# A graph network layer on one core: first edge layer in fp32 on 64 array rows per edge half, and its activation moved two units ahead of the messages

## What is computed

```
h    = relu(layernorm(x))                                  # per node
e    = relu(raw @ W_e1.T + b_e1) @ W_e2.T + b_e2           # per edge, raw has 64 features
edge = (e * (clip(polarity, 0, 1) + 0.01)) @ W_le.T + b_le
msg  = relu(h[src] + edge)
aggr = segment_sum(msg, dst)
u    = (h + aggr) @ W_g1.T + b_g1 ; layernorm with gain and bias ; relu
out  = x + u @ W_g2.T + b_g2
```

## Time and profile before

| | |
|---|---|
| median of 3 runs | 2511.51 us (2511.22 to 2516.98) |
| the profiled execution, its own time | 2513.17 us |
| its span in the profile | 2511.5 us |
| mean granted TensorE clock | 0.991 of full |
| PE busy | 2341.1 us, 93% |
| DVE busy | 1904.1 us, 76% |
| ACT busy | 1586.8 us, 63% |
| POOL busy | 1644.0 us, 65% |
| moved by DMA | 349.07 MB, mean 139 GB/s |

### The profile page before, as it was taken

The page is one execution under the profiler, slowest core; times in us unless marked ns, Lnnn a source line. Parts: engine busy times, 40 slices in busy tenths (PEclk is TensorE's granted clock), DMA queues, the critical chain, the costliest instruction groups (busy, mean ns, idle before and its releaser), DMA issues.

```text
span 2511.5 us, 34919 instructions
## 1 busy us (share of the span) xinstructions
PE 2341.1 (93%) x10492; PEld 1946.3 (77%) x10492; DVE 1904.1 (76%) x3747; ACT 1586.8 (63%) x3112; POOL 1644.0 (65%) x1679
## 2 busy tenths in 40 slices
PE   5798999999999999999999999999999999999998
PEld 4677787877887787778877787877787787787876
DVE  7677777877787777777777777777787777777776
ACT  7566666666666666666666666666666666666664
POOL 6666666666666666666666666666666666666663
PEclk9899999999999999999999999999999999999999
DMA  9444444444444444444444444444444444444442
GB/s 311 131 132 129 132 146 131 139 130 134 145 140 136 131 145 139 135 133 141 139 136 133 133 135 143 134 137 132 137 143 137 134 134 143 137 137 134 141 140 60
DMA packets 136344, 349.07 MB, mean 139 GB/s; under 512 B 32019, under 2 KB 58325, under 8 KB 136149
## 3 DMA queue, kind: packets, MB, share of 16 engines
q0 software_dynamic: 77376, 211.39, 29.6%
q1 hardware_dynamic: 58772, 135.37, 15.8%
HBM read 333.82 MB, written 12.82 MB: 138 GB/s over the span
## 4 chain that ended last, share of the span: by engine, by line
PE 50%; DVE 27%; another core or an unknown queue 9%; issue 9%; ACT 4%; POOL 1%; DVEq 0%; DMA 0%; ACTq 0%; SPq 0%
PE bank L828 29%; DVE bank L676 11%; PE bank L844 9%; DVE mhl L686 7%; PE bank L806 5%; DVE oh L665 4%; PE bank L807 4%; DVE rlo L427 3%; ACT mhl L601 1%; PE bank L875 1%; PE bank L861 1%; ACT rhi L422 1%; POOL x_sba L371 1%; ACT hh L589 1%
## 5 line engine op out<-in xcount | busy, mean ns | idle before, releaser
L578 POOL DMA_INDIRECT hx<-gather_table,sidx x1612 | 1604.9, 996 | 823.7 <-issue 400.6
L828 PE MATMUL bank<-wc,hh 128*128 128x256 f32 x6448 | 1467.2, 380 | 2.7 <-issue 2.5
L828 PEld LDWEIGHTS bank<-wc,hh 128*128 128x128 f32 x6448 | 1218.9, 191 | 179.8 <-issue 9.2
L601 ACT ACTIVATE mhl<-bank 128x512 fp32r<-128x512 f32 x806 | 482.3, 599 | 842.1 <-DVE bank L676 671.7
L676 DVE SCALAR_TENSOR_TENSOR bank<-bank,gt,hx 128x256 f32<-128x256 f32 x1612 | 683.0, 484 | 380.1 <-remote 311.1
L686 DVE SCALAR_TENSOR_TENSOR mhl<-bank,mhl 128x512 fp32r<-128x512 f32 x806 | 549.7, 689 | 26.8 <-ACT mhl L601 1.8
L806 PE MATMUL bank<-rhi,w1r 128*128 128x512 f32 x806 | 379.8, 471 | 129.2 <-ACT hh L589 81.7
L589 ACT ACTIVATE hh<-bank 128x512 f32<-128x512 f32 x806 | 441.2, 601 | 28.2 <-remote 19.4
L594 ACT COPY bank<-c 128x512 f32<-128x512 f32 x802 | 450.5, 609 | 0.0
L844 PE MATMUL bank<-mhl,oh 128*128 128x512 f32 x1612 | 444.0, 397 | 0.5 <-DVE mhl L686 0.5
L665 DVE TENSOR_TENSOR oh<-iota,slot 128x512 fp32r<-128x512 f32 x403 | 279.2, 693 | 138.6 <-PE bank L844 80.7
(11 more groups left out here) (93 smaller groups left out, 479.7 us busy)
## 6 DMA issues: line engine op xcount, KB each, us to landing
raw<-in_attr_m SPq DMA_DIRECT2D x202, 512.0 KB
hx<-gather_table,sidx POOLq DMA_INDIRECT x1612
x_sba<-in_x SPq DMA_DIRECT2D x12, 512.0 KB, 8.9
gather_table<-x_sba SPq DMA_DIRECT2D x12, 512.0 KB, 7.7
xt<-in_x SPq DMA_DIRECT2D x48, 128.0 KB
out<-xt SPq DMA_DIRECT2D x48, 128.0 KB
dst_i<-in_dst_m SPq DMA_DIRECT2D x1, 805.5 KB
sidx<-in_src_m SPq DMA_DIRECT2D x1, 805.5 KB
```

The source lines that it names most:

```text
L578: eng.indirect_dma_start(out=hx[:, u % NX, j, :], out_offset=None, in_=tables, in_offset=bass.IndirectOffsetOnAxis(ap=sidx[:, t:t + 1], ax ...
L601: eng.activation(mh[:, u % 2, 2 * q:2 * q + 2, :], LB[(2 * u + q) % 4][:, :].rearrange("p (j n) -> p j n", j=2), ACT.Relu).then_inc(r_mh, 1)
L828: last = eng.matmul(o, hh[:, u % 2, k, e0:e0 + P], wc[:, k, :], start=False, stop=(j == 1 and k == 1), skip_group_check=seeded)
```

## The change

The first layer is done in fp32 from the raw values. A unit's 512 edges lie as two halves of 256: the features of half 0 on rows 0 to 63, those of half 1 on rows 64 to 127. Four matmuls of 256 columns with 64 rows each replace the four of 512 columns with 128 rows; the halves alternate, and each half has a bank of its own. The two roundings (lines 422 and 427) go, with their tiles. The bias enters in the activation, which becomes four instructions of 256 columns. One load of raw values is one unit, and eight are kept. On ACT `hidden_high(u+2)` stands at the head of iteration u, and the seed of unit u+2 behind the messages of unit u. Some preparation of weights is gone, and the constant of the place at which SP handles a node tile is new.

```diff
-NR = 3
+NR = 8
-NM = 4
...
-                eng.wait_ge(s_w, 16 * len(loads))
-                eng.wait_ge(s_m, 6)
-                eng.tensor_copy(w1r[0:F, 0, :], w1[0:F, :])
-                eng.tensor_copy(w1r[F:P, 1, :], w1[F:P, :])
...
-        raw = sb("raw", [P, NR, 1024], F32, early)
-        rhi = sb("rhi", [P, NM, 512], F32R, early)
-        rlo = sb("rlo", [P, NM, 512], F32R, early)
+        raw = sb("raw", [P, NR, 256], F32, early)
...
-        def load_raw(eng, n):
-            eng.dma_start(raw[:, n % NR, :], attr_m[n, :, :]).then_inc(r_load[n % NR], 16)
-
-        def raw_high(eng, u):
...
-            eng.copy(rhi[:, u % NM, :], part(u)).then_inc(r_rh, 1)
-
-        def raw_low(eng, u):
...
-            eng.tensor_tensor(rlo[F:P, u % NM, :], part(u)[F:P], rhi[F:P, u % NM, :].bitcast(F32),
-                              ALU.subtract).then_inc(r_rl, 1)
+        def load_raw(eng, u):
+            eng.dma_start(raw[:, u % NR, :], attr_m[u, :, :]).then_inc(r_load[u % NR], 16)
...
-                hh = sb("hh", [P, 2, 2, 512], F32, c)
+                hh = sb("hh", [P, 2, 2, 2, D], F32, c)
...
-                    place = {(GU * g + 23) // 2: t for g, t in TILE_AFTER.items()}
+                    place = {GU * g + 27: t for g, t in TILE_AFTER.items()}
...
-                    for n in range(NR, (UNITS + 1) // 2):
-                        eng.wait_ge(r_rl, 2 * (n - NR) + 2)
+                    for n in range(NR, UNITS):
+                        eng.wait_ge(r_l1, 2 * (n - NR) + 2)
...
-                        for k in range(2):
-                            eng.wait_ge(r_l1, 2 * u + k + 1)
-                            eng.activation(hh[:, u % 2, k, :], LA[k][:, :], ACT.Relu).then_inc(r_hh, 1)
+                        for q in range(2):
+                            eng.wait_ge(r_l1, 2 * u + q + 1)
+                            for k in range(2):
+                                last = eng.activation(hh[:, u % 2, q, k, :], LA[q][:, D * k:D * k + D], ACT.Relu,
+                                                      bias=b1[:, k:k + 1])
+                            last.then_inc(r_hh, 1)
...
                     for u in range(UNITS):
-                        if u + 3 < UNITS:
-                            raw_high(eng, u + 3)
-                        if u + 1 < UNITS:
-                            hidden_high(u + 1)
+                        if u + 2 < UNITS:
+                            hidden_high(u + 2)
...
-                        if 1 <= u < UNITS - 1:
-                            seed(u + 1)
                         message_high(u, 0)
                         message_high(u, 1)
+                        if u + 2 < UNITS:
+                            seed(u + 2)
...
                     def first_layer(u):
-                        eng.wait_ge(r_rl, u + 1)
...
+                        loaded(eng, u)
+                        if u >= 1:
+                            eng.wait_ge(r_hh, 2 * (u - 1) + 2)
                         for k in range(2):
-                            if u >= 1:
-                                eng.wait_ge(r_hh, 2 * (u - 1) + k + 1)
-                            eng.matmul(LA[k][:, :], w1r[:, 0, k * P:k * P + P], rhi[:, u % NM, :], start=True, stop=False)
-                            eng.matmul(LA[k][:, :], w1r[:, 1, k * P:k * P + P], rlo[:, u % NM, :],
-                                       start=False, stop=True).then_inc(r_l1, 1)
+                            for h in range(2):
+                                last = eng.matmul(LA[h][:, D * k:D * k + D], w1[F * h:F * h + F, k * P:k * P + P],
+                                                  raw[F * h:F * h + F, u % NR, :], start=True, stop=True)
+                                if k == 1:
+                                    last.then_inc(r_l1, 1)
```

More of the change, by code:

```diff
@@ L158, in gpsimd @@
                 eng.wait_ge(s_z, 3)
-                eng.wait_ge(s_m, 6)
+                eng.wait_ge(s_m, 5)
                 eng.wait_ge(s_io, 2)
@@ L404, in gnn @@
         early = ExitStack()
[L405 to L428 removed]
+        raw = sb("raw", [P, NR, 256], F32, early)
+        def loaded(eng, u):
+            eng.wait_ge(r_load[u % NR], 16 * (u // NR + 1))
+        def load_raw(eng, u):
+            eng.dma_start(raw[:, u % NR, :], attr_m[u, :, :]).then_inc(r_load[u % NR], 16)
         def nodes_again():
@@ L536, in _ @@
                     load_raw(eng, 0)
+                    load_raw(eng, 1)
                     for g in b["stores"](eng):
@@ L540, in _ @@
                         if g == LATE:
-                            load_raw(eng, 1)
-                    load_raw(eng, 2)
+                            load_raw(eng, 2)
+                            load_raw(eng, 3)
+                    for u in range(4, NR):
+                        load_raw(eng, u)
                     eng.dma_start(wg1[:, :, :], W_g1T.rearrange("(k p) n -> p k n", p=P)).then_inc(s_wg, 16)
@@ L628, in _ @@
                     for g in b["scalar"](eng):
-                        if g == SPLIT:
-                            for u in range(2):
-                                raw_high(eng, u)
+                        pass
+                    eng.wait_ge(a["s_w"], a["n_w"])
                     eng.wait_ge(s_o1, 16 * FIRST)
                     hidden_high(0)
-                    raw_high(eng, 2)
-                    eng.wait_ge(s_wt, 2)
+                    hidden_high(1)
+                    eng.wait_ge(s_wt, 1)
                     for u in range(UNITS):
-                        if u + 3 < UNITS:
-                            raw_high(eng, u + 3)
-                        if u + 1 < UNITS:
-                            hidden_high(u + 1)
+                        if u + 2 < UNITS:
+                            hidden_high(u + 2)
                         t = TILE_AFTER.get(u // GU - 1)
@@ L739, in _ @@
                         pass
-                    raw_low(eng, 0)
-                    raw_low(eng, 1)
                     own = a["edges"](eng)
@@ L747, in _ @@
                         pass
-                    raw_low(eng, 2)
                     eng.wait_ge(s_sl, 1)
+                    eng.wait_ge(s_o1, 16 * FIRST)
                     onehot(0)
@@ L825, in second_layer @@
                                 o = LB[(2 * u + q) % 4][:, D * j:D * j + D]
-                                e0 = (2 * q + j) * P
                                 for k in range(2):
-                                    last = eng.matmul(o, hh[:, u % 2, k, e0:e0 + P], wc[:, k, :],
+                                    last = eng.matmul(o, hh[:, u % 2, q, k, j * P:j * P + P], wc[:, k, :],
                                                       start=False, stop=(j == 1 and k == 1), skip_group_check=seeded)
@@ L1205 @@
     p = "L0_gnn_"
-    tiles = (E + 1023) // 1024
-    attr_m = _np.zeros((tiles, P, 1024), _np.float32)
-    wide = _np.zeros((F, tiles * 1024), _np.float32)
+    wide = _np.zeros((F, UNITS * 512), _np.float32)
     wide[:, :E] = w["edge_attr_65"][:, 1:].T
-    attr_m[:, 0:F, :] = wide.reshape(F, tiles, 1024).transpose(1, 0, 2)
-    attr_m[:, F:P, :] = attr_m[:, 0:F, :]
+    attr_m = wide.reshape(F, UNITS, 2, 256).transpose(1, 2, 0, 3).reshape(UNITS, P, 256)
     data = [
```

20 lines of the change are left out of this document (removed).

## The result

The changed kernel takes **2636.5 us** (2632.7 to 2640.2, 4 runs), the kernel before 2512.9 us (2511.2 to 2517.0, 4 runs): ratio 1.0489, 95% interval 1.0468 to 1.0511. It is slower by 124 us. 2480 us was forecast, with a range of 2395 to 2720.

What follows compares the result with a forecast made beforehand. PE was taken as the bound, 93% busy. Passes removed -371, new passes +435, shape changes +20, idle -115 sum to -31 us: from 2513.2 to 2482 profiled, 2480 us as median; range 2395 to 2720, its own 2400 to 2505.

Steps and rivals of the forecast that it cites:

- the rivals: Slower cases: serial first-layer passes 2716 us (0.22), dear shape changes 2591 us (0.20), no gain from ACT's order 2595 us (0.06).
- the round trip between 128 and 64 rows: PE, around each unit's first layer: changing array rows and back costs 0.05 us, 20 us in all; high end 282 us.
- the order on ACT: ACT: hidden values no longer stand behind late messages, so PE's 114.0 us idle before the first layer should nearly go.
- the 115 us: PE idle before the first layer, with weight loads exposed at restarts, taken off by ACT's new order; range 0 to 140.
- five slots: PE, new first layer: eight fp32 passes on two row halves overlap into five slots, 1.08 us a unit, 435 us.
- rival 4: PE, new first layer: halves overlap wholly, four slots, 348 us, total 2348 us; chance 0.52 together with the forecast.
- the 371 us removed: PE, old first layer: four fp32r passes a unit go, 0.92 us x 403 units.
- if a pass may start as soon as the one ahead has started: PE, new first layer: program order, with its own rows free, sets when a pass starts; gives 1.08 us a unit.
- Rival 2: PE, around the first layer: overlap as forecast, but 0.17 to 0.70 us a round trip; 2591 us with 0.35; chance 0.20.
- The reserve at the seed: ACT: time to spare before PE needs the seed of unit u+2 at T+7.5, T ending second_layer(u); 2 us or more.
- 0.1 us or more at either change of shape: Sign that the forecast is wrong: this much standing on PE where it goes between 128 and 64 rows.
- DVE busy some 1,625 us: Sign for the forecast: DVE's busy time after losing its rounding, line 427, 279 us.

Runs made afterwards that it cites:

- full_rows: Changed kernel, lift ahead of hidden_high(u+2), half 1 left out from unit 1 on, its two first-layer matmuls on all 128 rows: 2310.6 us.
- halves_in_turn: Changed kernel, lift ahead of hidden_high(u+2), both first-layer matmuls of half 0 issued before both of half 1: 2469.0 us.
- lift_first: Changed kernel with the node tile's lift put ahead of hidden_high(u+2) on ACT: 2467.0 us; 2546.7 us on the chip with late signals.
- eight_full: Changed kernel, lift ahead of hidden_high(u+2), the same four first-layer matmuls on all 128 rows, eight passes: 2651.3 us.

## Why the prediction was wrong

It forecast a small gain and the kernel lost 124 us; the time lies in the wide range, on the side of the rivals. The step that failed most is the round trip between 128 and 64 rows, taken at 0.05 us and 20 us in all: it is 0.38 us and 152. The second is the account of the order on ACT: the 115 us were put down to an order that by itself wins nothing, and the node tile's wait that it brings, 72 to 90 us, was left out. Step by step:

**The passes: right, at the lower bound.** The sum took five slots for 435 us. It is four slots, 348 us, rival 4's; together with the 371 us removed that makes -23, and `full_rows` shows -26. The detail that failed is "if a pass may start as soon as the one ahead has started": each row half goes its own way (`halves_in_turn`). The Trainium skill ("TensorE: Matmul & The Clock Gate", Part 3) says that matmuls on different row groups run concurrently. The trace agrees, with pairs 0.007 us apart.

**The change of shape: the term that was mis-sized.** I took 0.05 us for a round trip, 20 us in all; it is 0.38, 152 us. Rival 2 had it, between 0.17 and 0.70. Rows 7 had something of its size: the detour over one column and back cost 0.33 us above the normal pitch, and I explained it away, first by two weight loads of 0.08, then by a wait for "issue". [0.37 <-issue] there looks like [0.33 <-issue] at every change of rows here, a weight load that isn't let ahead; no run took that detour alone, so that it is the same thing is argued. Read as one, 0.33 x 403 = 133 us in place of 20 would have turned the sum from -31 to +82. In the trace the next load starts 0.31 us after the last pass has started, which is 0.09 after that pass's 0.216 are over; then the load itself is exposed, 0.10 from 1203.80 to the true start of line 770 (its eighth start less three pitches, 1203.80 + 1.13 - 0.38 - 0.65 = 1203.90). Both together are the 0.19. The Trainium skill ("TensorEngine Tiling (Array Packing)", Key Properties) says that a change of tiling mode drains TensorE. The trace agrees in that nothing of the new shape starts within the 0.216 us of the last pass of the old one; how much of the 0.09 is a drain it can't show.

**The order on ACT: the wait went, but not for the reason given, and one wait was left out.** The idle before the first layer went from 114.0 to 5.2 us, as forecast. What that was worth, and whether it was the order, is told below. The reserve at the seed was misread as 2 us or more; by the step's own times it is T+7.5 less T+6.0 at worst, 1.5; nothing here hung on it. But the step followed hidden values, messages and seed, and no other instruction behind the moved one. `hidden_high(u+2)` waits for PE's first layer, and behind it on ACT stands the lift of a node tile, for which PE waits in the same unit. Timeline of ACT and then of PE in the changed kernel:

```profile
593.11 1.57 ACT L559 ACTIVATE hh<-bank,b 128x256 f32<-128x256 f32 x4 [1.92 <-PE bank L770]
594.56 0.83 ACT L594 ACTIVATE rt<-bank,lnb,lng 128x128 f32<-128x128 f32 x2
```
```profile
592.00 1.21 PE L806 MATMUL bank<-mhl,oh 128*128 128x512 f32 x4
595.44 0.58 PE L836 MATMUL bank<-g2r,onr 128*128 128x256 f32 x1 [2.23 <-ACT rt L594]
595.82 1.91 PE L837 MATMUL bank<-wg,rt 128*128 128x256 f32 x4
597.52 4.13 PE L790 MATMUL bank<-wc,hh 128*128 128x256 f32 x16
```

ACT waits until 593.11, does four activations, and the lift begins at 594.56; PE, which ran out of work at about 593.2, starts at 595.44. After the idle its clock is at the lower of its two levels: the granted clock from 595.4 to 598 is 0.50 of full, line 837's four passes took 1.91 us there (0.43 a pass where 0.216 is normal) and line 790's sixteen 4.13 where 3.62 is normal. The granted clock of the whole run is 0.983 against 0.991. Moving the lift gives back 72 us where signals are in time, and 90 where they are late.

**The sum again,** for the chips of the first measurement: 2513 - 23 + 152 - 115 + 90 = 2617 us. 2636.5 were measured. Most of the missing 20 us lie in the 115, which is too much. By the totals late signals cost the kernel before 2513.8 - 2336.3 = 177 us and `lift_first` 2546.7 - 2467.0 = 80, so the change took off 98. With 98, the -26 of `full_rows` and the 4 us of half 1 the sum is 2513 - 26 + 152 + 4 - 98 + 90 = 2635. Where the signals come in time it is 2336 - 26 + 152 + 4 + 72 = 2538, and 2539 was measured. As most of these terms are differences of the same runs, that the sums close is no proof of its own; it shows that no great term is missing.

**Is the gain the order's?** By these runs, no. In the kernel before the order removes the wait before the first layer (114.0 to 10.1) but as much comes up elsewhere, and the time goes up by 27 us. In the new kernel with added lateness both orders cost the same, and both suffer 90 us or more less from late signals than the kernel before does with either order. So what made the kernel less sensitive lies in the rest of the change, with the roundings gone and a unit that lasts 0.35 us longer on PE; which of these does it stays open. That 98 us came off where 115 were forecast is luck, not the mechanism of the forecast. The new kernel with the old order wasn't run on such a chip without the addition.

Of the signs named beforehand, "0.1 us or more at either change of shape" came true, and PE does wait at the segment, though for 9.6 us only; "DVE busy some 1,625 us" was 1584; the wait at line 836 was not on the list.

## What to carry to other kernels

Going from full array rows to half and back cost 0.38 us of TensorE each time here, however well the halves overlap inside. Set that against what the overlap saves: eight passes on two row halves cost 184 us less in all than eight on full rows (`lift_first` against `eight_full`), round trips included. They lost here because they replaced four fp32r passes that needed no change of rows. When an instruction that waits is moved ahead in an engine's order, list everything that now stands behind it and who waits for that, the once-in-a-group work included. And a gain that consists of idle time is only worth what that idle is on the chip at hand: look whether its cause is in the program, and test the part that is to win it by itself.

## What the runs showed of the hardware

The same program, the kernel before, with the same matmul pitch of 0.216 us, takes 2336 us on three chips and 2514 on a fourth, run after run within 0.3%. In the profiles with the long time PE's signals often reach the other engines 1 to 4 us after the recorded end of the matmul, now and then later. DVE's totals on the slow chip, in the new kernel with the lift first:

```profile
L645 DVE SCALAR_TENSOR_TENSOR bank<-bank,gt,hx 128x256 f32<-128x256 f32 x1612 | 678.2, 484 | 381.0 <-remote 335.6 <-PE bank L790 34.7 <-DMA hx<-gather_table,sidx 7.6
```

335.6 us for "remote", while on the other chips this line never waits for it, only for PE and now and then for a gather. Late gathers can't be all of it: ACT's hidden values need nothing but PE, and they wait in the same way in this run (us in total, times, longest), while none of its waits for DVE is put down to "remote":

```profile
ACT hh L559 <- remote: 310.9, 112, 8.4
```

The cause was not found. It made the change look better than it is: it hit the kernel before for 2513 - 2336 = 177 us, the changed one for 2636.5 - 2539 = 97.

Also new to me: matmuls on the two halves of the array's rows run side by side even where the program puts them in sequence (`halves_in_turn`, 1.14 us for eight passes), and the change of rows costs the same 0.19 us in fp32 and in fp32r.
